# Another order of the first steps, and tile 0's work two steps later, in a masked-attention layer

## The reference

```python
mask = adj + eye(n)
q, k, v = (h @ W.T + b for each), split into 8 heads
scores = einsum('nhd,mhd->hnm', q, k) / sqrt(32), -1e9 where mask == 0
ctx = einsum('hnm,mhd->nhd', softmax(scores), v)
h1 = layer_norm(h + ctx @ Wo.T + bo)
h2 = layer_norm(h1 + relu(h1 @ W1.T + b1) @ W2.T + b2)
```

## Time and profile before

| | before |
|---|---|
| median of 3 runs | 551.26 us (550.77 to 552.02) |
| profiled execution | 551.33 us, its span 549.5 us |
| PE busy | 477.5 us, 87% of the span |
| DVE busy | 386.4 us, 70% |
| POOL busy | 278.7 us, 51% |
| ACT busy | 219.8 us, 40% |
| DMA moved | 92.18 MB in 43131 packets |

### The profile page before, as it was taken

One profiled execution on the slowest core, in us unless ns is written; L12 is line 12 of the kernel. 1 busy time (PEld: TensorE's weight loads), 2 busy tenths in 40 slices (PEclk: granted clock), 3 DMA queues, 4 the chain that ended last, 5 costly groups with the idle time before them and its releaser, 6 DMA issues.

```text
span 549.5 us, 7452 instructions
## 1 busy us (share of the span) xinstructions
PE 477.5 (87%) x2306; PEld 378.6 (69%) x2306; DVE 386.4 (70%) x1066; ACT 219.8 (40%) x547; POOL 278.7 (51%) x384
## 2 busy tenths in 40 slices
PE   5999996973669999999999999989786898989993
PEld 4888885863445885785787687578445777878782
DVE  0558679556295898999899899698777478975103
ACT  1233342331336246336245434743642525354430
POOL 7554341441084267776777546426465267761202
PEclk9999997897679999999999999999898988989998
DMA  7999988999379969979997956375465756420001
GB/s 178 295 267 271 260 277 296 223 289 164 122 106 262 177 120 245 152 260 154 247 271 101 248 151 117 104 143 113 109 108 154 141 113 183 127 79 19 20 0 42
DMA packets 43131, 92.18 MB, mean 168 GB/s; under 512 B 4936, under 2 KB 21192, under 8 KB 42960
## 3 DMA queue, kind: packets, MB, share of 16 engines
q0 software_dynamic: 16512, 55.60, 52.0%
q1 hardware_dynamic: 24784, 34.22, 17.7%
q10 hardware_dynamic: 1792, 1.85, 1.0%
HBM read 123.61 MB, written 16.80 MB: 256 GB/s over the span
## 4 chain that ended last, share of the span: by engine, by line
PE 53%; DVE 17%; DMA 10%; issue 7%; ACT 7%; POOL 3%; SPq 1%; POOLq 0%; ACTq 0%; DVEq 0%
PE ps L1115 16%; PE ps L1128 13%; DMA xT_all<-in_xT 8%; PE ps L1827 5%; PE ps L1095 4%; DMA q_table<-slots 3%; PE ps L869 2%; PE ps L1843 2%; DVE adj_bytes L529 2%; PE ps L1083 2%; PE ps L831 2%; DVE adj_bytes L525 1%; PE ps L872 1%; PE ps L1105 1%; ACT xT_all L1169 1%
## 5 line engine op out<-in xcount | busy, mean ns | idle before, releaser
L1115 PE MATMUL ps<-xT_all,w 128*128 128x512 f32 (+1 forms) x320 | 123.7, 535 | 3.5 <-ACT xT_all L1169 2.9
L1128 PE MATMUL ps<-w,xT_all 128*128 128x256 f32 x512 | 121.9, 393 | 3.1 <-ACT xT_all L1169 3.1
L1128 PEld LDWEIGHTS ps<-w,xT_all 128*128 128x128 f32 x512 | 98.2, 197 | 16.8 <-ACT xT_all L1169 3.8
L1115 PEld LDWEIGHTS ps<-xT_all,w 128*128 128x128 f32 x320 | 61.3, 202 | 46.5 <-issue 35.1
L1038 POOL DMA_INDIRECT slots<-kv_table,col_of x54 | 55.0, 1018 | 71.9 <-DVE col_of L613 60.6
L1028 POOL DMA_INDIRECT slots<-kv_table,found x48 | 53.1, 1106 | 55.8 <-PE ps L872 31.5
L1169 ACT ACTIVATE xT_all<-ps,col_table 128x512 f32<-128x512 f32 (+1 forms) x80 | 47.8, 603 | 61.9 <-PE ps L1115 61.9
L1827 PE MATMUL ps<-early,xT_all 128*128 128x256 f32 x256 | 59.3, 393 | 6.4 <-DMA early<-in_wqkvT 6.2
L1827 PEld LDWEIGHTS ps<-early,xT_all 128*128 128x128 f32 x256 | 49.9, 197 | 14.3 <-DMA xT_all<-in_xT 4.7
L525 DVE MAX8 adj_bytes<-adj_bytes 128x8 f32<-128x1024 f32 (+5 forms) x40 | 38.2, 974 | 19.0 <-DMA adj_bytes<-in_adj 19.0
L1046 POOL DMA_INDIRECT work<-q_table,row_of x40 | 42.7, 1069 | 15.3 <-issue 13.3
(11 more groups left out here) (176 smaller groups left out, 861.1 us busy)
## 6 DMA issues: line engine op xcount, KB each, us to landing
adj_bytes<-in_adj POOLq DMA_DIRECT2D x31, 512.0 KB, 10.4
kv_table<-slots POOLq DMA_DIRECT2D x7, 1024.0 KB, 14.3
xT_all<-in_xT SPq DMA_DIRECT2D x13, 512.0 KB, 19.6
slots<-kv_table SPq DMA_DIRECT2D x12, 512.0 KB, 12.1
q_table<-slots SPq DMA_DIRECT2D x16, 256.0 KB, 7.6
q_own<-q_table SPq DMA_DIRECT2D x12, 256.0 KB, 15.4
out_dram<-early SPq DMA_DIRECT2D x6, 512.0 KB, 3.8
slots<-in_adj SPq DMA_DIRECT2D x1, 2048.0 KB, 24.7
```

The costliest lines, as they stand in the source:

```text
L1115: last = nc.tensor.matmul(ps[:, q["bank"] + f % 2, 0:q["g"] * P], w1[:, k, f * P:(f + 1) * P], q["h1T"][:, k, :], start=(k == 0), stop=(k ...
L1128: nc.tensor.matmul(to, q["ffT"][:, f, j * P:(j + 1) * P], w2[:, f, :], start=(f == 0), stop=False)
```

## The change

1. **Phase one, SP.** After the first query store and the own rows of step 0, SP waits until step 0's gathered edges and queries have landed, and only then stores further query pairs. The own rows of step 1 come after store 1. The dense weights and the load of x for the first dense job go behind the own rows of step 2; x goes ahead of the weights.
2. **Query pairs.** 8 stages in place of 4 (the new four lie in a spare part of the mask buffer). Nine pairs are made before step 0 (six before), five in step 0, two in step 1.
3. **POOL.** Step 0's aligned gathers come after its edges and queries. Of the mask loads for three steps ahead the first is issued before `gather_edges`, the second after `gather_queries`; before, both were at the end.
4. **PE and DVE around step 0.** `starts_pe` of tile 0 comes one pair earlier, the searches of steps 1 and 2 are interleaved with tile 0's lists, and step 1's lists and masks (ACT too) come before the last query pairs.
5. **Tile 0.** `GATHER0, SCORE0` go from 2, 4 to 4, 6. The 7 scored pieces are in steps 6 to 12, the softmax in step 13 and the weights in steps 14 and 15; the sum stays in step 16.

```diff
-GATHER0, SCORE0 = 2, 4
+GATHER0, SCORE0 = 4, 6
...
+        Q_STAGES = 8
...
+        row0 = spare[:, STAGE_AT - TILE0.U:STAGE_AT]
         q_stage = [slots[2][:, i, :] for i in range(STAGES)]
+        q_stage += [spare[:, STAGE_AT + i * 2 * D:STAGE_AT + (i + 1) * 2 * D] for i in range(Q_STAGES - STAGES)]
...
-        Q_BEFORE = 6
+        Q_BEFORE, Q_LISTS = 9, 6
...
-                return ((6,), (), (7, 8), (9, 10), (11,), ())[gap]
-            return ((12,), (), (13,), (14,), (15,), ())[gap] if i == 1 else ()
+                return ((9,), (10,), (11, 12), (13,), (), ())[gap]
+            return ((14,), (15,), (), (), (), ())[gap] if i == 1 else ()
...
             store_q(0)
             load_own(sp, STEPS[0])
-            for i in range(1, Q_BEFORE):
+            sp.wait_ge(got_edges[STEPS[0].par], 2 * STEPS[0].U * 16)
+            store_q(1)
+            load_own(sp, STEPS[1])
+            for i in range(2, Q_BEFORE):
                 store_q(i)
...
-                if i + 1 < NB:
+                if 1 <= i < NB - 1:
                     load_own(sp, STEPS[i + 1])
...
-                        sp.wait_ge(s_q_ps, Q_BEFORE)
+                        sp.wait_ge(s_q_ps, 4)
...
                 if soon:
                     gather_aligned(pool, soon)
+                if i + 3 < NB:
+                    load_adj(pool, STEPS[i + 3].h)
...
-                if i + 3 < NB:
-                    for ti in range(STEPS[i + 3].T):
-                        load_adj(pool, STEPS[i + 3].h + ti)
+                if i + 3 < NB and STEPS[i + 3].T > 1:
+                    load_adj(pool, STEPS[i + 3].h + 1)
...
             for q in STEPS[S:]:
...
+                if 0 <= i - SCORE0 < PIECES0:
+                    queries0_pe(pe, i - SCORE0)
...
+                if 0 <= i - SCORE0 < PIECES0:
+                    ell0_pe(pe, i - SCORE0)
```

More of the change, by code:

```diff
@@ L311, in build @@
         s_q = sem("s_q")
-        s_q_out = [sem(f"s_q_out{i}") for i in range(STAGES)]
+        s_q_out = [sem(f"s_q_out{i}") for i in range(Q_STAGES)]
         adj_loaded = [sem(f"adj_loaded{i}") for i in range(BUFFERS)]
@@ L821, in starts_pe @@
             wait(pe, distance, 2 * q.p)
+            if q.b == 1 and not q.first:
+                pe.wait_ge(cols_ready, TILE0.p + 1)
             nc.tensor.matmul(ps[:, SMALL, 0:q.U], minus_before[:], units(spill, q), start=True, stop=True).then_inc(starts_ps, 1)
@@ L827, in lists_pe @@
             wait(pe, cols_ready, q.p)
-            if q.b == 1 and not q.first:
-                pe.wait_ge(onehot0_ready, 1)
             for u in range(q.U):
@@ L1484, in _ @@
                 n, place, count = step_of_job(q)
-                if i + 1 < NB:
+                if 1 <= i < NB - 1:
                     load_own(sp, STEPS[i + 1])
-                if i == 0:
+                if i != 1:
+                    for gap in range(6):
+                        for p in q_pairs(i, gap):
+                            store_q(p)
+                if i == 2:
+                    load_own(sp, TILE0)
+                if place == 1 and q.group <= WIDE_JOBS:
+                    if q.group == 0:
+                        sp.wait_ge(s_q_ps, 4)
+                    wait(sp, main["attn_ps"], q.group)
+                    post_load(sp, JOBS[q.group], q.group, JOBS[q.group]["t"])
+                if i == 1:
                     for dst, src in ((wo, woT.rearrange("(k p) n -> p k n", p=P)), (w1, w1T.rearrange("(k p) n -> p k n", p=P)),
@@ L1492, in _ @@
                         sp.dma_start(rows[name][:], src.to_broadcast([P, D])).then_inc(s_weights, 16)
-                for gap in range(6):
-                    for p in q_pairs(i, gap):
-                        store_q(p)
-                if i == 2:
-                    load_own(sp, TILE0)
-                if place == 1 and q.group <= WIDE_JOBS:
-                    if q.group == 0:
-                        sp.wait_ge(s_q_ps, Q_BEFORE)
-                    wait(sp, main["attn_ps"], q.group)
-                    post_load(sp, JOBS[q.group], q.group, JOBS[q.group]["t"])
+                    for gap in range(6):
+                        for p in q_pairs(i, gap):
+                            store_q(p)
                 if i == S + 2:
@@ L1699, in _ @@
             mask_act(act, TILE0)
-            for i in range(1, Q_BEFORE):
+            for i in range(1, Q_LISTS + 1):
+                take_q(i)
+            distance_act(act, STEPS[1])
+            mask_act(act, STEPS[1])
+            for i in range(Q_LISTS + 1, Q_BEFORE):
                 take_q(i)
@@ L1762, in _ @@
                     onehot_act(act, soon)
+                if i == SOFTMAX0:
+                    probs0_act(act)
                 if i == S:
@@ L1858, in _ @@
                     project_q(0)
-            starts_pe(pe, TILE0)
-            for i in range(1, 4):
+                if i == 14:
+                    starts_pe(pe, TILE0)
+            for i in range(1, Q_LISTS):
                 project_q(i)
             lists_pe(pe, TILE0)
-            for i in range(4, Q_BEFORE):
+            project_q(Q_LISTS)
+            starts_pe(pe, b1_)
+            for i in range(Q_LISTS + 1, Q_BEFORE):
                 project_q(i)
-            starts_pe(pe, b1_)
             for q in STEPS[:S]:
```

58 lines of the change are left out of this document (31 added, 27 removed).

## The result

The changed kernel takes 558.08 us (median of 4 runs, 553.29 to 561.92), the kernel before 551.64 us beside it (4 runs, 550.77 to 552.27): ratio 1.0096, 95% interval 1.0062 to 1.013, so **+5.3 us**, slower. The forecast was 556.2, +4.9. In a second comparison it is 558.24 (6 runs, 554.02 to 560.76) against 551.16 (20 runs), ratio 1.012 (1.0087 to 1.0153). Its runs scatter over 7 to 9 us, those of the kernel before over 1.5 to 4. A ratio leaves disturbed runs out and a median here doesn't, so the two can differ by a few us (one run of the kernel before, beside experiments 5, 6, 8 and 10, took 729 us).

A forecast was written before the change was run, and what follows sets the result against it. It took full DMA engines to bound 75 to 141 us, PE 207 to 386, and engine handovers 386 to 430. +3.2 - 3.5 + 5.2 = +4.9 us on 551.3 gave 556.2 us, range 546.0 to 560.0.

The forecast's parts named there:

- first part: Steps 0 to 2: first dense matmul of step 2 near 145.5 us, before 142.29; +3.2 us.
- the landing: Arrival of the dense weights ahead of step 2's dense work: near 144.6 us, 3.8 us past 140.8.
- one more mask load in front, +5.0: Steps 0 to 2: a fifth mask load, on POOL's queue, comes ahead of the weights' arrival, costing +5.0 us.
- the hold's loss: 75 to 84 us: SP holds query stores until step 0's gathers land, so 0.5 MB is missing there; +1.4 us.
- The forecast's premise: 75 to 141 us: full DMA engines set step 2's dense start, so transfers count, not issue times.
- my first rival: SP's issue sets the weights' arrival; two mask loads fewer in front, 134.6 us, total 546.2 us; chance 0.13.
- Second part: Steps 4 and 5 each lose a scored piece of 1.76 us of PE; -3.5 us, at the least -2.
- Third part: Steps 11 to 14, with tile 0's last scored pieces, softmax and weights moved later: +5.2 us, bounds 0 and +8.
- Step 12: A scored piece ahead of its own masks makes its probabilities, and PE's L1105 behind them, 2.4 us later.
- +8, if the new waits also lower the clock: Upper bound for steps 11 to 14, should the granted clock fall as in 386 to 430 us (0.84).
- Step 13: It gets the softmax, so the values for PE's sum come later; +2.8 us.
- Step 14: 3.2 us more on PE and 3 us on DVE fit into their waits there; no cost.

The follow-up runs named there:

- experiment 5: Kernel before with tile 0's gathers, scores, softmax and weights one step later (GATHER0, SCORE0 = 3, 5): 560.62 us, ratio 1.0171.
- experiment 6: Kernel before with tile 0's scores one step later (5 to 11), softmax at 13 and weights at 14, two steps later: 557.87 us, ratio 1.013.
- experiment 8: Changed kernel with 12 matmuls whose result nobody reads put ahead of step 12's transposes: 558.05 us, ratio 1.0134.
- experiment 10: Kernel before with the first wide job's load of x issued on SP ahead of the stores of query pairs 6 to 15: 537.75 us, ratio 0.9757.
- experiment 4: Changed kernel with both mask loads of a step behind the gather of the queries again: 559.33 us, ratio 1.0133.
- experiment 11: The order only kernel with dense weights, then x, issued on SP in step 0 ahead of query pair 9: 550.46 us, ratio 0.9969.
- experiment 12: The experiment 11 kernel with the stores of query pairs 11 to 13 moved to step 1, behind step 2's own rows: 547.15 us, ratio 0.9943.
- order only: Changed kernel with tile 0's gathers, scores, softmax and weights back at their old steps (GATHER0, SCORE0 = 2, 4): 552.43 us, ratio 1.0019.
- Tile 0 only: Kernel before with only tile 0's parts moved two steps later (GATHER0, SCORE0 = 4, 6): 557.58 us, ratio 1.0065.
- experiment 7: Kernel before with only tile 0's weights moved from steps 12 and 13 to 14 and 15: 554.2 us, ratio 1.0039.

## Why the prediction was right, and where it was not

The sum was +4.9 and the result +5.3, but by parts it was **first part +3.2 forecast, about +1 measured; second and third together +1.7 forecast, +3.6 (ratio) to +6.4 (median) measured**. Two errors of opposite sign made the total look better than its terms: that it came within 0.4 us is luck.

*First part.* Right: DVE reached step 0 sooner (88.1 against 89.7), five mask loads had been issued when the weights landed, DMA stayed full, PE stood from 123 us on. Wrong: the landing, 141.5 to 143.5 in place of 144.6, and the term **"one more mask load in front, +5.0"**. I counted all transfers from 75 us on. What hardly varied is the time from SP's issue, 35.5 to 36.3 us in five profiles and 38.1 in the sixth, and taking one load away didn't bring the landing forward (experiment 4). The first load was issued at 85.9 in place of 100.9, just behind the stretch in which SP's hold leaves the engines partly idle (DMA 0.63 in 75 to 84 us); that it was so paid from time that I had booked as the hold's loss is argued. The forecast's premise that the full engines bound the start of the dense work, whatever the order on SP, fell with experiment 10, though experiments 11 and 12 show that an earlier start can be lost again behind it; my first rival named the mechanism (SP's issue sets the landing), but for this change SP issues the weights 19 us later than before (107 against 88), and that undoes what x's earlier place wins. The Trainium skill's rule of turns between queues ("DMA: Bandwidth & Descriptors", Queues, rings and completion order) is not at odds with that: two queues share, and within SP's queue the order is what the kernel chose. No run here tests the rule itself.

*Second part.* Forecast -3.5 for steps 4 and 5, measured +0.5 for the two: this step failed. From DVE's first operation of a step to the next, order only against the changed kernel, step 5 gave 0.6 (22.9 to 22.3 us) and step 4 took 1.1 more (23.1 to 24.2). PE's rows of step 4, first order only, then the changed kernel:

```profile
186.07 0.55 PE L848 MATMUL ps<-work 128*128 128x56 f32 x4
187.34 1.10 PE L1100 MATMUL ps<-wo,xT_all 128*128 128x256 f32 x4 [0.72 <-issue]
...
188.50 1.03 PE L1100 MATMUL ps<-wo,xT_all 128*128 128x256 f32 x4
```

```profile
184.73 0.63 PE L848 MATMUL ps<-work 128*128 128x56 f32 x4
186.94 1.31 PE L1100 MATMUL ps<-wo,xT_all 128*128 128x256 f32 x4 [1.59 <-issue]
...
188.47 1.92 PE L1100 MATMUL ps<-wo,xT_all 128*128 128x256 f32 x4
```

The piece stood ahead of a wait; without it the wait is 0.87 us longer, and behind it the matmuls of 1.03 us take 1.92. Tile 0 only and the changed kernel's second profile have the same rows (a wait of 1.58 us, then 1.91 to 1.92) and the same 24.3 us for step 4. PE's share of 97% hid that the removed matmuls were not on the path. (The stretch that I took it from, 207 to 342 us, begins with step 5; step 4 lies before it.)

*Third part.* Its sum was nearly right without the clock, and its terms were not: forecast 2.4, 2.8 and 0 for steps 12, 13 and 14, measured 1.3, 2.6 and 1.8. Step 12: PE idle "3 to 4 us ahead of L1105" was right (3.67), and so was the reason given, that the 28 transposes stood just ahead of that wait. The term +2.4 measured 1.3 (13.95 against 12.66 us), 1.0 of it the piece. What it left out of the sum and had only in a bound ("+8, if the new waits also lower the clock") is as large as any term: +1.7 us in experiment 7 and +2.6 in the changed kernel's second profile, and it fell in 5 of 7 profiles with the wait. Step 13: +2.8 forecast, 2.6 measured (from step 12's transposes to step 14's first wide output product 34.10 us, before 31.47), with the 1800-element passes on the chain as forecast:

```profile
398.00 2.04 DVE top_rec L785
400.06 2.03 DVE scores L787
...
404.61 1.94 DVE total_p L793
```

Softmax 13 against weights 14, the same but for the softmax and one step of the scores, gives 557.87 - 554.20 = 3.7 us (5.0 by the ratios). Step 14, **"nothing"**, was wrong: from its first wide output product to its transposes it takes 15.24 us in the changed kernel and in the kernel with only the weights at 14, before 13.42, so 1.8 us. The gathers ahead of POOL's normalization come as soon after the first wide output product as before (7.6 us in both). The difference is in one operation of POOL, which DVE's pass over tile 0's weighted values holds up by 1.64 us (experiment 7). I had looked at step 14 for idle time on PE and DVE that would take in the new work, and not at what the new pass on DVE stands beside.

## What to carry to other kernels

Work that is taken from a busy engine wins only if nothing behind it was waiting: read the row behind the removed one first. Before you call the idle time of a step a home for more work, read what POOL does while DVE would run the new pass. Where DMA engines are full, don't count bytes for a start time: ask which transfer is the last that its user waits for, when it is issued, and how much its own queue has outstanding then. One load of 512 KB moved ahead of ten stores was worth 13 us here, while the larger reordering, which moved it too and put 2.6 MB of weights and rows behind it, was worth nothing. Compare more than one profile of a kernel before you give a place 2 us. And when a forecast agrees with the result, run its parts alone.

## What the hardware showed that I had not expected

- An operation of POOL on 128x2 elements took 1.32 to 1.84 us in place of 0.20 beside a DVE product of two tensors over 128x1792 elements (2.01 us), and ended with it: in nine profiles of nine where the two met in step 14, in none of five where they didn't.
- A wait of 3.49 us or more in step 12 was followed by transposes at about half speed (1.97 against 1.04 to 1.09 us) in 5 of 7 profiles, a shorter one in none of 7, with the same program falling on either side (5.85 or 8.40 us for the same instructions). In two of the seven without the wait the products right ahead of the transposes ran at the lower clock.
- On a full queue an own-row load of 256 KB took 21.2 us from issue to landing, and SP stood 16.7 us in the issue of one row of 128 KB.
- In one profile each of two kernels of the changed order DVE stood 7.35 us near 80 us in place of 3.65, for a reason that no row names. One of them has a median 4.6 us higher than a kernel that differs by six matmuls at 380 us (562.63 against 558.05).
